# Turning row maxima onto their own partitions: four wide transposes and a ScalarE eviction in place of one transpose and a transfer

## The reference, cut to what matters

```
qkv = (x @ qkv_w).reshape(b, n, 3, H, D)
scores = jnp.einsum('bhnd,bhmd->bhnm', q, k) * scale
scores = jnp.where(mask, scores, -jnp.inf)
attn = jax.nn.softmax(scores, axis=-1)
out = jnp.einsum('bhnm,bhmd->bhnd', attn, v)
x = x + gate_msa[:, None, :] * _modulate(_layernorm(out @ proj_w + proj_b), shift_msa, scale_msa)
x = x + gate_mlp[:, None, :] * _modulate(_layernorm(_mlp(x)), shift_mlp, scale_mlp)
```

## Time and profile before

| | us |
|---|---|
| median of 3 runs (1421.8 to 1427.55) | 1422.58 |
| the profiled execution, its own time | 1422.82 |
| its span in the profile | 1421.0 |
| PE busy within the span | 1298.0 |
| second block, from its first pair of scores to its last transposes to tokens | 872.4 to about 1370 |

### The profile page before, as it was taken

One profiled execution on the slowest core, in us unless ns is written; L12 is line 12 of the kernel. 1 busy time (PEld: TensorE's weight loads), 2 busy tenths in 40 slices (PEclk: granted clock), 3 DMA queues, 4 the chain that ended last, 5 costly groups with the idle time before them and its releaser, 6 DMA issues. The chain is left out here.

```text
span 1421.0 us, 24552 instructions
## 1 busy us (share of the span) xinstructions
PE 1298.0 (91%) x8789; PEld 994.6 (70%) x8789; DVE 798.7 (56%) x2240; ACT 765.3 (54%) x1262; POOL 755.1 (53%) x939
## 2 busy tenths in 40 slices
PE   4899999999999999999999996989888888888887
PEld 3577777777787788777787785666666666565656
DVE  3766746746646646647646544464564646464452
ACT  3466665765765765756755753454535444454432
POOL 3698867867877777777777751021322224041323
PEclk9899999999999999999999998999999999999988
DMA  8432322322323313213314316363425243332100
GB/s 259 138 117 56 87 86 53 98 75 67 99 60 84 94 49 90 91 44 91 100 36 111 112 25 185 99 181 87 163 58 163 78 138 101 114 130 74 46 2 30
DMA packets 98259, 133.98 MB, mean 94 GB/s; under 512 B 16802, under 2 KB 51498, under 8 KB 98130
## 3 DMA queue, kind: packets, MB, share of 16 engines
q1 hardware_dynamic: 96850, 131.80, 31.8%
q10 hardware_dynamic: 1280, 0.53, 0.1%
HBM read 72.64 MB, written 58.75 MB: 92 GB/s over the span
## 5 line engine op out<-in xcount | busy, mean ns | idle before, releaser
L1398 DVE CUSTOM_DVE_ANT_0 shifted<-score,bias 128x512 f32<-128x512 f32 x512 | 332.1, 686 | 259.8 <-PE score L869 138.3
L631 POOL TENSOR_SCALAR shifted<-shifted,row_max 128x512 f32<-128x512 f32 x512 | 359.6, 714 | 200.7 <-DVE row_max L1398 199.0
L1109 ACT ACTIVATE probs<-turned 128x512 f32<-128x512 f32 x512 | 277.7, 595 | 222.6 <-PE turned L881 222.0
L881 PE MATMUL turned<-ident,shifted 128*128 128x128 f32 x2048 | 270.2, 275 | 6.4 <-POOL shifted L631 6.0
L881 PEld LDWEIGHTS turned<-ident,shifted 128*128 128x128 f32 x2048 | 232.5, 141 | 59.6 <-issue 28.9
L797 PE MATMUL dense<-w_down,hidden 128*128 128x256 f32 x1024 | 255.0, 381 | 0.8 <-ACT hidden L1090 0.8
L624 POOL TENSOR_SCALAR bias<-dist,scale 128x1024 f32<-128x1024 f32 x192 | 217.2, 1132 | 14.0 <-DMA down_bias<-in_L_cond_b 14.0
L869 PE MATMUL score<-k_rows,q_rows 97*128 97x512 f32 x512 | 202.4, 457 | 13.7 <-DMA k_rows<-mask_neg 4.3
L797 PEld LDWEIGHTS dense<-w_down,hidden 128*128 128x128 f32 x1024 | 180.3, 190 | 31.0 <-issue 9.6
L777 PE MATMUL dense<-feat_m,w_up 128*128 128x512 f32 x768 | 191.1, 401 | 3.4 <-ACT hidden L1090 1.8
L777 PEld LDWEIGHTS dense<-feat_m,w_up 128*128 128x128 f32 x768 | 144.5, 192 | 37.3 <-ACT hidden L1090 5.2
(11 more groups left out here) (138 smaller groups left out, 1546.4 us busy)
## 6 DMA issues: line engine op xcount, KB each, us to landing
qk_rows<-qk_high SPq DMA_DIRECT2D x128, 256.0 KB
q_rows<-qk_rows SPq DMA_DIRECT2D x64, 384.0 KB
qk_rows<-qk_low SPq DMA_DIRECT2D x64, 256.0 KB
k_rows<-qk_rows SPq DMA_DIRECT2D x68, 192.0 KB
x_in_t<-in_x SPq DMA_DIRECT2D x8, 512.0 KB, 4.8
x_res<-in_x SPq DMA_DIRECT2D x8, 512.0 KB, 5.7
x_mid<-x_norm SPq DMA_DIRECT2D x8, 512.0 KB, 3.2
x_in_t<-x_mid SPq DMA_DIRECT2D x8, 512.0 KB, 3.9
```

The lines of the kernel that those rows point to most:

```text
L631: ins = pool.tensor_scalar(shifted[:, u % 3, i, :], shifted[:, u % 3, i, :], -1.0, row_max[:, t % 6:t % 6 + 1], ALU.mult, ALU.add)
L881: mm = pe.transpose(turned_bank[z % 2][:, HALF * kk + P * i:HALF * kk + P * i + P], shifted[:, u % 3, i, P * kt:P * kt + P], ident[:, :])
L1109: act.activation(probs[:, u % RING, 2 * pair:2 * pair + 2, :], turned_bank[z % 2][:, :].rearrange("p (a c) -> p a c", a=2), ACT.Exp)\
L1398: dve.tensor_tensor_reduce(shifted[:, u % 3, i, :], score_bank[t % 2], bias[:, u % 2, i, :], 1.0, 3.0e38, ALU.add, ALU.min, row_max[:, t % ...
```

## The change

The maxima are written into a wide tensor, `wide_peak`, 128 x 4 x 101, which lies in the memory of `no_bias` (unused on the short path). For each of the four tiles of 128 queries it has 101 columns, of which the last four take that tile's maxima, high and rest for both heads. Columns 0 to 95 are set to 0 and column 96 to -1 once, at the start, by two memsets of DVE. T(q) becomes four transposes, which put 101 rows x 512 into bank 0, with the maxima already on partitions 97 to 100. ACT copies partitions 96 to 100, times -1, straight into `q_rows` (row 96, the row of ones, is written again as 1). `take_peaks` on DVE, the transfer by ACT, and the tensors `split_peak` and `peaks` go. S(q+1) and U(q) now both wait for ACT's copy.

```
-        split_peak = sb("split_peak", [P, 4 * TT], F32R)
-        peaks = sb("peaks", [4 * TT, P], F32R)
+        wide_peak = no_bias[:, 0:TT * ALL_ROWS].rearrange("p (t c) -> p t c", t=TT)
...
             def turn_peaks(n, q):
                 pe.wait_ge(s["split_ready"], H // 2 * (n - B) + q + 1)
-                pe.transpose(score_bank[0][0:4 * TT, 0:P], split_peak[:, :].bitcast(F32), ident[:, :])\
-                    .then_inc(s["peak_turned"], 1)
+                for t in range(TT):
+                    mm = pe.transpose(score_bank[0][0:ALL_ROWS, P * t:P * t + P], wide_peak[:, t, :],
+                                      ident[:, :])
+                mm.then_inc(s["peak_turned"], 1)
...
             def turned_scores_of(n, q):
-                pe.wait_ge(s["peaks_loaded"], 16 * (H // 2 * (n - B) + q + 1))
+                pe.wait_ge(s["peaks_ready"], H // 2 * (n - B) + q + 1)
...
-            def load_peaks(n, q):
+            def peaks_out(n, q):
                 g, pair = q // 2, q % 2
-                act.wait_ge(s["peaks_ready"], H // 2 * (n - B) + q + 1)
-                act.dma_start(q_rows[PEAK_AT:ALL_ROWS, g, pair, :].bitcast(F32), peaks[:, :].bitcast(F32))\
-                    .then_inc(s["peaks_loaded"], 16)
+                act.wait_ge(s["peak_turned"], H // 2 * (n - B) + q + 1)
+                act.activation(q_rows[MASK_AT:ALL_ROWS, g, pair, :], score_bank[0][MASK_AT:ALL_ROWS, :], ACT.Copy,
+                               scale=-1.0).then_inc(s["peaks_ready"], 1)
...
             def peaks_of(n, q):
+                if count == 1:
+                    dve.wait_ge(s["wide_set"], 2)
-                parts = split_peak[:, :].rearrange("p (a x t) -> p a x t", a=2, x=2)
+                parts = wide_peak[:, :, PEAK_AT:ALL_ROWS].bitcast(F32R).rearrange("p t (a x) -> p a x t", x=2)
...
-            def take_peaks(n, q):
-                count = H // 2 * (n - B) + q
-                dve.wait_ge(s["peak_turned"], count + 1)
-                if count > 0:
-                    dve.wait_ge(s["peaks_loaded"], 16 * count)
-                dve.tensor_scalar(peaks[:, :], score_bank[0][0:4 * TT, 0:P], -1.0, None, ALU.mult)\
-                    .then_inc(s["peaks_ready"], 1)
...
+                dve.memset(wide_peak[:, :, 0:MASK_AT], 0.0).then_inc(s["wide_set"], 1)
+                dve.memset(wide_peak[:, :, MASK_AT:ALL_ROWS], -1.0).then_inc(s["wide_set"], 1)
```

More of the change, by code:

```diff
@@ L259, in build @@
                  "res_ready0", "res_ready1", "scaled", "y_ready", "y_stored", "scale_step", "row_ones", "peak_high",
-                 "split_ready", "peak_turned", "peaks_ready", "peaks_loaded", "mean_minus", "norm_shift_ready", "normed",
+                 "split_ready", "peak_turned", "wide_set", "peaks_ready", "mean_minus", "norm_shift_ready", "normed",
                  "y_scaled", "y_done", "last_ready", "tile_stats0", "tile_stats1", "tile_mean0", "tile_mean1", "tile_var0",
@@ L1174, in turn @@
                         if 2 <= p < 2 + H // 2:
-                            load_peaks(n, p - 2)
+                            peaks_out(n, p - 2)
                         if 3 <= p < 3 + H // 2:
@@ L1523, in turn @@
                             dense(piece, m)
-                        if 2 <= p < 2 + H // 2:
-                            take_peaks(n, p - 2)
                         for piece, m in pieces(HEADS, 3 * p + 2, n):
```

## The result

The changed kernel takes 1437.89 us in the median (1436.37 to 1438.88, 4 runs) against 1422.44 us before in the same runs: a ratio of 1.0093, 95% interval 1.0073 to 1.0113. That is 0.9% slower, as forecast (1435.6 us). The profiled execution took 1436.37 us with a span of 1434.6.

The account below looks back on a forecast made before the run. PE, busy 91%, was taken to bound the kernel. Transposes +21.1, hand-over +9.0, transfer -15.6 and clock -1.7 sum to +12.8 us on 1422.82: 1435.6 us, 0.9% slower, own range 1429 to 1443, full range 1421 to 1449.

Parts of the forecast that it names:

- The four transposes: T(q) on PE's path: three more transposes, 0.33 us a pair over 64 pairs, +21.1 us.
- The hand-over: From T(q) to S(q+1): ACT's copy replaces DVE's eviction, 0.39 us longer where uncovered; +9.0 us after absorption.
- absorbed by the wait for GELU behind S(2): PE's wait for ACT's GELU after 18 matmuls behind S(2) takes up 0.4 us a turn of the longer hand-over.
- The other absorption: L948 at pairs 3 and 5 waits 0.33 us for exponentials; half, 0.17 us twice, absorbs the hand-over.
- The transfer: U's waits on PE for the transferred maxima, pairs 2, 4, 6 and the like, go: -15.6 us.
- U(7), costed at nothing: U(7) comes soon after T(7) but waits for ACT's exponentials of pair 6 as before: 0 us.
- The clock: The half-clock stretch after the 3.03 us transfer wait at pair 2 goes: -1.7 us.
- Costed at nothing: DVE's 64 fewer instructions (17.7 us) and end of waits for T gain nothing; two memsets at the start hidden.
- The signs named: Copy near 0.60 us; S about 1.37 after T; U's idle at most 0.84; last turn 3 us longer, others less.
- the wait was all real: Rival: U's weight loads' 39.4 us idle are all lost to the transfer; faster, 1412 us; chance 0.10.
- the hand-over is hidden: Rival: 5-row copy near 0.3 us, or most of 0.39 absorbed; no change, 1427 us; chance 0.20.
- The clock falls more often: Rival: thinner stretches from pair 3 to 7 cost one more half-clock stretch each turn, +14, 1449 us; chance 0.10.

Follow-up runs that it names:

- the short copy: Changed kernel with ACT's copy cut to the first 128 of 512 columns: 1421.14 us, ratio to before 0.9985.
- the first experiment: Kernel before without the 64 transfers of the maxima, U waiting for DVE's eviction only: 1407.64 us, ratio 0.9876.
- the pause filled: Changed kernel with one projection of six matmuls (qk 3) moved ahead of T(0) on all engines: 1428.17 us, ratio to before 1.0034.
- shortening the hand-over at five pairs: Changed kernel with S's two matmuls into bank 1 first, before the wait for the copy: 1427.20 us, ratio to before 1.0022.
- with both: Changed kernel with qk 3's projection ahead of T(0) and S's two matmuls into bank 1 first: 1416.26 us, ratio to before 0.9950.
- the short copy and one transpose: Changed kernel with one wide transpose instead of four and the copy cut to its 128 columns: 1409.68 us, ratio 0.9909.

## Why the prediction was right, and where its steps were off

The time and the sign were right, and the main mechanism as well: work on PE and a longer hand-over against a wait of some pairs. That the sum came within 2.3 us of the median is in part luck: the transfer took 3.5 us more off than forecast and the transposes cost 2.2 less, and the clock, which went the other way by 6.0, made up for both. The steps, by the ruler, from the kernel before to the changed one:

- **The four transposes**: forecast +21.1 us at 0.33 a pair. Starts are 0.11 us apart, as read from L956. By the runs +19.2 in the kernel before; by the ruler 15.8 in seven gaps and 0.39 x 8 = 3.1 in the first (8.13 against 7.74 where the clock was full), 18.9. Right; the missing 2.2 us are the 0.14 us that ACT's GELU covers at pairs 1 and 2.
- **The hand-over**: forecast +9.0, measured +12.8 at the five pairs less 4.1 of absorption at pair 1, +8.7. Its pieces were off in ways that cancelled. ACT starts 0.04 us behind PE, not 0.11, so the copy's excess was 0.32 and not 0.39, and 1.60 us a turn instead of 1.86. The 0.4 us that I took as absorbed by the wait for GELU behind S(2) was right in kind, and 0.51 in size: S(2) comes 0.63 us later after T(1), yet T1-T2 grew by 0.12 only, and the wait is gone. That ACT "is otherwise no later than before" holds: from T(1)'s weight load to the table load ahead of the exponentials it takes 1.47 us against 1.60, as the copy stands where the issue stood. The other absorption failed. The 0.33 us before L948 at pairs 3 and 5, of which I took half, is a lag of the weight load: in the changed kernel it stands there 24 times, with no releaser, and the short copy shortened these gaps by the full 0.32.

```profile
PEld pv L952 <- issue: 8.0, 24, 0.3
```

- **The transfer**: forecast -15.6. The three pairs gave -15.3, and the weight loads' remaining idle time is the 24 x 0.84 that was subtracted. U(7), costed at nothing, was wrong: it was a landing too, 3.4 us without a transfer, of which the changed kernel keeps 0.9, as the rest goes to the transposes. With 0.4 in the other gaps the term was -19.1. ACT's issue, 4.1 us on PE's path at pair 1, I had not seen as a cost; it is the same wait for GELU that stands above as absorbed, and counts once.
- **The clock**: forecast -1.7, and this step failed, in sign too. T0-T1 was at half clock in 3 of 8 turns before and in 6 of 8 after: 74.8 - 8 x 8.13 = 9.7 us against 67.4 - 8 x 7.74 = 5.4, so +4.3. The stretch behind the late transfer of turn 12 did go, worth at least the 1.0 us by which its T3-T4 (4.52) stood above the others; the ruler counts that 1.0 outside T0-T1, with the gaps of the transfer.
- **Sum**: outside T0-T1, -23.2 (transfer and issue gone) + 0.4 (ACT for DVE, short) + 15.8 + 12.8 = +5.9; in T0-T1 +3.1 and +4.3. That is 13.3 us in the profiles (in the forecast's own terms 18.9 + 8.7 - 19.1 + 0.4 + 4.3). The medians differ by 15.5; about 2 us of this lie between the profiled executions and the medians, as the changed kernel's was the shortest of its four, 1.5 us under the median, and that of before 0.4 above.
- **Costed at nothing**: right for DVE's 14.8 us; nothing shows in the totals for the memsets either.
- **The signs named**: the copy's 0.589 us and S waiting for ACT came as forecast, S starts 1.28 to 1.37 us after T where nothing covers it, and U's weight loads idle no more than 0.84. But the last turn was to be longer by 3 us or more and the others by less. By the ruler it grew by 2.6, turn 9 by 4.1 and turn 8 by 2.8: turn 15 was at half clock before and after, and turn 9 only after, which is the clock's step again.

Of the rivals, "the wait was all real" fell with the first experiment, "the hand-over is hidden" with the copy's 0.589 us and with the short copy. "The clock falls more often" came true in part: three more falls, at T(0), not one in every turn between pairs 3 and 7. The Trainium skill's rule in "TensorE: Matmul & The Clock Gate", section on PE-mode transpose, that transposes do not count as busy the way matmuls do, was not needed for it: with one transpose instead of four the falls at T(0) were more (8 of 8), and with the pause filled and all four transposes there they were gone in turns 9 to 14.

## What to carry to other kernels

When a transfer is replaced by an engine's instruction, count where the instruction is waited for at once: here the transfer was waited for a step later and hidden in most pairs, and the copy sits between T and S in five of eight. A gap of weight-load idle time behind short-weight passes is a lag and not a wait; the proof is that it stays where nothing is late. A longer hand-over can be partly paid by a wait that follows it: look whether what ends that wait is itself held up. And the pause before T(0) cost its length and then, in some turns, a stretch at half clock, so filling it was worth about as much (9.7 us) as shortening the hand-over at five pairs (10.7 us): with both, the same change came out 0.5% faster than the kernel before.

## What the hardware showed that I had not expected

- The same pause of 1.4 us before T(0) was followed by half clock in 3, 6, 7, 4 and 8 of 8 turns in the kernel before, the changed one, without the transfer, with the short copy, and with the short copy and one transpose. A kernel made shorter elsewhere can lose several us there; what decides in which turns, I have not found.
- ACT's copy of 5 rows takes as long as one of 128 rows: 0.589 us for 512 columns against 0.597, and 0.269 for 128 columns. DVE takes 0.697 for 5 x 512 and 0.276 for 16 x 128.
- From the issue of a transfer of 8 KB to the matmul that waits for it, it took 1.87 us with the DMA engines 1% busy over 1110 to 1112 and 6.55 us where they were 95% busy for part of the time.
